# Cross-attention kernel: order of the key and value parts in the folded context rounds, and where round six's value weights are made

## The reference, cut to what matters

```
h_k = (key_value_states @ w_k.T).reshape(b, lk, 32, 128)     # 1024 context tokens, 512 -> 32 heads x 128
h_v = (key_value_states @ w_v.T).reshape(b, lk, 32, 128)
score = einsum('bqhd,bkhd->bhqk', h_q, h_k) + position_bias  # later, and not touched
```

## Time and profile before

| | |
|---|---|
| median of three runs | 1600.57 us |
| the profiled execution | 1600.67 us, its span 1598.9 us |
| TensorE (PE) busy | 1588.5 us, 99% of the span |
| VectorE / ScalarE / GpSimd busy | 1035.0 / 771.3 / 886.6 us |
| ten folded halves | from 51.17 to 248.41 us |

### The profile page before, as it was taken

How to read it: one execution, slowest core, us unless ns; L and a number is a source line. 1 busy time by engine, 2 the same in 40 slices (tenths; PEclk the granted TensorE clock), 3 DMA queues, 4 the chain that set the end, 5 groups by cost and what they waited for, 6 DMA issues and landing times.

```text
span 1598.9 us, 25827 instructions
## 1 busy us (share of the span) xinstructions
PE 1588.5 (99%) x8872; PEld 1375.3 (86%) x8872; DVE 1035.0 (65%) x1568; ACT 771.3 (48%) x1952; POOL 886.6 (55%) x688
## 2 busy tenths in 40 slices
PE   9999999999999999999999999999999999999999
PEld 7899998888888888888888887888888898889887
DVE  7455546746666666666778667767656656665675
ACT  5233334534545545445544334656555546564563
POOL 6455554456664765755569776454536445443435
PEclk9999999999999999999999999999999999999999
DMA  9444444323333333333332111111111111010011
GB/s 353 168 159 158 157 158 164 149 79 98 119 113 107 119 102 108 124 96 108 114 128 60 46 41 51 60 34 47 41 33 30 44 41 34 27 47 27 14 54 53
DMA packets 57395, 146.49 MB, mean 92 GB/s; under 512 B 7425, under 2 KB 22401, under 8 KB 56801
## 3 DMA queue, kind: packets, MB, share of 16 engines
q1 hardware_dynamic: 57312, 145.41, 26.8%
HBM read 107.64 MB, written 37.75 MB: 91 GB/s over the span
## 4 chain that ended last, share of the span: by engine, by line
PE 95%; DVE 2%; POOL 1%; ACT 1%; issue 1%; DMA 0%; SPq 0%; DVEq 0%; ACTq 0%
PE banks L55 27%; PE banks L57 27%; PE banks L56 27%; PE banks L866 4%; PE banks L886 4%; PE banks L2505 4%; PE banks L875 2%; PE banks L2512 2%; PE banks L224 1%; DMA rawA<-in_x_wK 0%; DVE resid L2155 0%; DVE s_centred L1309 0%; PE banks L808 0%; DVE g_q L2805 0%; DMA g_swapped<-in_l_b 0%
## 5 line engine op out<-in xcount | busy, mean ns | idle before, releaser
L2969 POOL TENSOR_TENSOR g_swapped<-g_swapped,rawB 128x512 f32<-128x512 f32 x80 | 103.0, 1290 | 171.1 <-ACT g_swapped L2651 171.1
L1747 POOL TENSOR_TENSOR x_probs<-x_probs,x_inv 128x512 f32<-128x512 f32 x64 | 66.6, 1041 | 169.3 <-DVE x_inv L1531 166.5
L1183 ACT ACTIVATE x_probs<-x_probs,x_top 128x128 f32<-128x128 f32 x256 | 100.2, 392 | 92.1 <-DVE x_top L1522 92.1
L1647 POOL TENSOR_TENSOR wtA_lo<-rawA,wtA_hi 128x1024 fp32r<-128x1024 f32 (+1 forms) x31 | 72.3, 2332 | 79.6 <-ACT wtB_hi L1050 55.3
L2799 DVE TENSOR_TENSOR g_turned_by<-banks,rawB 128x512 f32<-128x512 f32 x80 | 55.2, 690 | 86.2 <-ACT g_swapped L2651 86.2
L2963 POOL TENSOR_TENSOR g_probs<-g_probs,g_inv 128x512 f32<-128x512 f32 x64 | 67.7, 1079 | 74.7 <-DVE g_inv L2790 74.5
L2650 ACT COPY g_swapped<-banks 64x512 f32<-64x512 f32 x80 | 46.8, 585 | 120.1 <-PE banks L57 113.3
L55 PE MATMUL banks<-wtV_hi,g_att_lo 128*128 128x512 f32 x256 | 104.2, 407 | 0.0
L55 PE MATMUL banks<-xT_hi,wtO_lo 128*128 128x512 f32 x256 | 102.9, 402 | 0.0
L56 PE MATMUL banks<-wtV_lo,g_att_hi 128*128 128x512 f32 x256 | 100.3, 392 | 0.0
L57 PE MATMUL banks<-xT_hi,wtO_hi 128*128 128x512 f32 x256 | 100.2, 391 | 0.0
(11 more groups left out here) (388 smaller groups left out, 5267.5 us busy)
## 6 DMA issues: line engine op xcount, KB each, us to landing
kept_k<-c_k_kept SPq DMA_DIRECT2D x16, 1024.0 KB, 4.0
x_k<-kept_k SPq DMA_DIRECT2D x32, 512.0 KB, 4.5
x_v<-kept_v SPq DMA_DIRECT2D x28, 512.0 KB, 3.7
kept_v<-c_v_kept SPq DMA_DIRECT2D x20, 512.0 KB, 3.9
rawA<-in_x_wQ SPq DMA_DIRECT2D x16, 512.0 KB, 4.5
rawO<-in_x_wO SPq DMA_DIRECT2D x16, 512.0 KB, 3.5
rawO<-in_g_wQ SPq DMA_DIRECT2D x16, 512.0 KB, 3.5
rawV<-in_g_wO SPq DMA_DIRECT2D x16, 512.0 KB, 3.5
```

The costliest lines, as they stand in the source:

```text
L1183: e = nc.scalar.activation(probs[:, b, :], probs[:, b, :], ACT.Exp, bias=top[:, b:b + 1], accum_out=total[:, b:b + 1])
L1647: return pool.tensor_tensor(wt[into][1][:, cut], raw[kind][:, cut], f32(wt[into][0][:, cut]), ALU.subtract)
L2969: pool.tensor_tensor(part, part, sin[:, :].unsqueeze(1).to_broadcast([P, HB, P]), ALU.mult)\
```

## The change

TensorE issues a folded half in the order K1 to K5, V1 to V4, K6 K7, V5 V6 V7. The other engines' queues follow: ScalarE's second key copy (`key_quarter`) goes ahead of the first value copy, its key weights behind the cast of V and of the combined value weights; VectorE's sums are put in the same new order. The V and O weights of round six are made in the second half of round five (`plain_weights` on ScalarE, `value_weights(i + 1)` behind the key weights on GpSimd), and round six's first key copy goes ahead of `scale_x(1)`.

```
@@ tensor, folded_half
                 key_start(i, j)
+                key_middle(i, j)
                 if j == 0:
                     weights_ready("V", i + 1)
...
                 value_part(Y, vs2, ct2, j)
-                key_middle(i, j)
                 value_part(Z, vs1, ct1, j)
-                key_end(i, j)
                 pe.wait_ge(vo_added, group_added(m) + 1)
                 value_part(Y, vs3, ct3, j, True)
+                key_end(i, j)
@@ scalar
+            def plain_weights(i, kind, used):
+                act.wait_ge(vo_made, used)
+                split(kind, i + 1).then_inc(w_hi[kind], 1)
...
                         key_copy(i, j)
+                        key_quarter(i, j)
                         value_copy(i, j)
-                        key_quarter(i, j)
                         if more:
                             folded_weights(i + 1, "V", group_made(m) + 3)
-                        key_weights(m + 1)
+                        elif j == 1:
+                            plain_weights(i + 1, "V", group_made(m) + 3)
                         if more:
                             second_third_high(i + 1, group_made(m) + 4)
+                        key_weights(m + 1)
                         value_quarter_copy(i, j)
                         if more:
                             folded_weights(i + 1, "O", group_made(m) + 6)
                             fourth_high(group_made(m) + 7)
+                        elif j == 1:
+                            plain_weights(i + 1, "O", group_made(m) + 6)
                     return
-                value_weights(i)
                 scale_x(0)
+                key_copy(i, 0)
                 scale_x(1)
-                key_copy(i, 0)
@@ vector, value_sums: rest() is split after the sums of V4 and of Z into following() and last()
+                        next_two()
                         value_first()
                         if more:
                             value_combine_more(i + 1)
-                        next_two()
+                        value_next()
                         last_two()
-                        value_rest()
+                        value_last()
@@ gpsimd
-                if isinstance(i, int) and i == QUADS - 2:
-                    value_weights(i)
...
-                if not isinstance(i, int) or i < FOLDED:
-                    value_weights(i + 1)
-                if isinstance(i, int) and i == QUADS - 2:
-                    value_weights(QUADS - 1)
+                value_weights(i + 1)
```

More of the change, by code:

```diff
@@ L1361, in first, with following @@
                     value_sum(v01, Y, v10)
-                def rest():
+                def following():
                     dve.wait_ge(vo_made, group_made(m) + 4)
@@ L1367, in rest, with last @@
                     value_sum(v11, Z, v11)
+                def last():
                     dve.wait_ge(vo_made, group_made(m) + 6)
@@ L1372, in rest @@
                     value_sum(v01, Z, v01)
-                return first, rest
+                return first, following, last
             f11, f21, f12, f22 = (halves(raw[kind][:, :])[:, :, 2 * P * f:2 * P * (f + 1)] for kind in "VO" for f in range(2))
@@ L1441, in context_round @@
                         first, next_two, last_two = key_sums(i, j)
-                        value_first, value_rest = value_sums(i, j)
+                        value_first, value_next, value_last = value_sums(i, j)
                         if j == 0:
```

## The result

The changed kernel takes 1611.25 us, the median of four runs (1611.23 to 1611.3), against 1600.3 us before (four runs, 1599.77 to 1600.83): a ratio of 1.0067, 95% interval 1.0056 to 1.0079. It is 10.95 us slower; the forecast was 1610.9 us, in a range of 1608.0 to 1614.0. The profiled execution has a span of 1609.5 us, 10.6 more than before.

The account below looks back on a forecast made before the run. TensorE, busy 99% of the span, was taken to bound the kernel. Halves +12.1 and round six -1.8 gave +10.3 us on 1600.67, 0.1 less on the median's scale: 1610.9 us, range 1608.0 to 1614.0.

Parts of the forecast that it names:

- The cover of 0.42 us: Folded halves before: four value parts behind K7 take 5.75 us, 0.42 us longer than the key weights' chain of 5.33.
- The sum for the halves: Waits before the next K1 in ten folded halves: 9 x 1.25 + 0.86 = 12.1 us more.
- The upper bound of 0.42 us a half: Release before K1: at most the 0.42 us between GpSimd's end and K1, making a half at most 1.5 us longer.
- Round six: K4's wait on the key copy in round six goes: -1.8 us, with ends of 0 and -1.8.
- rival (c): Round six: port order goes the other way, GpSimd's V before the centring; 1612.2 us; forecast with (c) 83%.
- Rival (a): Folded halves: key weights are not late, only the gains are left; 1598.2 us, faster by 0.15%; 5%.
- Rival (b): Folded halves: stalls come and ScalarE's later cast of B adds +2 to +4 us; 1613 to 1615 us; 10%.
- Rival (d): Context stage: new waits lower TensorE's granted clock, ten times 0.5 us more; 1616 us; 2%.

Follow-up runs that it names:

- the second edit alone: Kernel before with only round six's V and O weights made in round five and its key copy ahead of scale_x(1): 1599.58 us, before 1600.64.
- The run with longer waits: Changed kernel with K6 and K7 one value part later still (K1 to K5, V1 to V5, K6 K7, V6 V7): 1641.18 us, before 1600.81.

## Why the prediction was right

- **The cover of 0.42 us was the number that decided.** K7 was to end 15.35 us into a half and did at 15.35 plus the restart of 0.09; the chain behind it was to be 5.33 us and was 5.30. Moving K7 back by one value part took the stalls away, one part later made them longer, and a shorter chain behind it at the same place took most of them away. That is shown from both ends. But the 0.42 us were not free, as the prediction took them to be: the time from GpSimd's end to K1 goes off them too, and inside the loop it is 0.34 us or more. At 90.89 us, the first K1 inside the loop, the kernel before was already at the edge: K1 stood 0.36 us behind B's low part, and its first matmul took the 0.33 us of a restart.
- **The sum for the halves was 12.1 us, and it was 12.76.** The term that was mis-sized is TensorE's start behind GpSimd, taken as 0.15 us from the earlier trace rows. It was 0.10 or 0.11 us at four K1s, 0.34 or 0.35 at five, and 0.51 at the first K1 inside the loop: 2.6 us in all instead of 1.5. The upper bound of 0.42 us a half was meant for this (one start went past it), and written-out rounds show that the loop is the reason. Against that, B's low part was ready a little sooner than reckoned, 0.45 us over the ten halves. The upper end of the prediction's own sizes, +14.6 us, is 1615.2 us and lies outside the range that it gave.
- **Round six gave 1.70 us where 1.8 were predicted.** The number is right in part by luck. The prediction put all of it down to the second edit, and of the 1.70 us the order alone gives 1.14. The centring got in ahead of GpSimd's V as I argued, with 0.13 us to spare. With the second edit alone it didn't, and 1.12 us were won. So rival (c) is real; it was the stall that kept it away here. Its price was set too high: the wait at K5 was 0.38 us and not 1.3, and 1.12 us were left of the gain and not 0.5.
- **Rival (a)**, key weights not late, is out: the ten halves take 20.75 to 21.28 us each.
- **Rival (b)**, ScalarE adding to the stalls, didn't happen: B's cast waits 0.28 to 0.30 us for K7 with ScalarE idle in all ten halves, those with combined value weights too, and inside the loop the second halves are as long as the first ones (21.09 against 21.05 to 21.08 us).
- **Rival (d)**, a lower clock behind the waits, didn't happen in the changed kernel: 1.00 in all its halves. I put it aside with "nothing in the trace speaks for it". The run with longer waits shows that it is real: ten waits of 2.3 to 2.6 us brought it in every time, those of 0.9 to 1.4 us never did. The Trainium skill (TensorE: Matmul & The Clock Gate, Part 1) says that TensorE's activity decides between 1.2 and 2.4 GHz; the two levels are the ones in the rows above.

## What to carry to other kernels

With one buffer for the next stage's weights, the last reader of that buffer starts a chain, and what stands behind it in the queue is its cover. Measure that chain from the reader's end to the last writer's end, add the time that the waiting engine takes to start (0.10 to 0.51 us here), and compare it with the cover before moving the reader; here 5.33 us stood against 5.75, and one part of 1.44 us taken out of the cover cost 1.3 us in each of ten halves. If the order must change, shorten the chain: a second signal, so that the first half of the work starts with its own input, gave back 10 of 11 us.

An edit that is worth 1 or 2 us at one place should be timed alone. This one was worth 1.12 us in round six by itself and 0.56 us on top of the new order, since the order had freed part of the same wait and changed who came first at the shared port.

## What the runs showed of the hardware that was not expected

- The start of TensorE behind a GpSimd operation took 0.10 us in code written out, and 0.34 us inside the hardware loop, with the same two instructions (0.51 us at the loop's first K1).
- After waits of 2.3 to 2.6 us TensorE ran at the 0.50 clock for about 3 us, at all ten K1s of that kernel, at a cost of some 1.46 us each beyond the wait. After the waits of 0.9 to 1.4 us in the changed kernel it never did, and neither after the one of 1.50 us in the kernel before.
- VectorE and GpSimd stood still for each other's whole operation when both had two inputs in SBUF: a centring of 0.74 us took 2.92, and in the other direction GpSimd's V took 3.39 us instead of 2.40 in the changed kernel. When GpSimd had a second operation queued, the waiting VectorE operation went in between the two: in the earlier trace rows it ran 1.08 us of its 2.14 us there, and GpSimd's next took 3.40 us instead of 2.41.
